# A conv block and a window-attention layer on one core: loads put ahead of stores, and four places in the strip order changed

## What is computed

```python
# L0: 1x1 conv (128->64), 3x3 grouped conv, 1x1 conv (64->128), each with its norm
h = relu(bn(conv(x, w1))); h = relu(bn(conv3x3(h, w2))); x = relu(bn(conv(h, w3)) + x)
# L1: windows of 7 x 7 = 49 tokens, shifted by 3; 8 heads of 16 channels
y = roll(ln(x) * w + b, (-3, -3)); win = windows(y)            # 8 windows in a strip of 7 rows
q, k, v = split(win @ qkv_w.T)
p = softmax(q @ k.T * scale + bias + mask)
x = x + roll(unwindow((p @ v) @ proj_w.T + proj_b), (3, 3))
z = ln(x) * w2 + b2
out = x + gelu(z @ fc1_w.T + fc1_b) @ fc2_w.T + fc2_b
```

## Time and profile before

| what | us |
|---|---|
| median of 3 executions | 4834.04 (4832.89 to 4839.28) |
| the profiled execution | 4831.1 |
| its span | 4829.0 |
| TensorE busy (matmul) | 4439.0 (92%) |
| ScalarE busy | 3444.2 (71%) |
| VectorE busy | 3214.6 (67%) |
| GpSimd busy | 2213.1 (46%) |

### The profile page before, as it was taken

One profiled execution on the slowest core, in us unless ns is written; L12 is line 12 of the kernel. 1 busy time (PEld: TensorE's weight loads), 2 busy tenths in 40 slices (PEclk: granted clock), 3 DMA queues, 4 the chain that ended last, 5 costly groups with the idle time before them and its releaser, 6 DMA issues.

```text
span 4829.0 us, 192181 instructions
## 1 busy us (share of the span) xinstructions
PE 4439.0 (92%) x71190; PEld 3280.4 (68%) x71190; DVE 3214.6 (67%) x7717; ACT 3444.2 (71%) x5644; POOL 2213.1 (46%) x3242
## 2 busy tenths in 40 slices
PE   8999996999999999999999999999999999999998
PEld 5666665666667666667666666666666666677665
DVE  4343435777777777777777777777777777777775
ACT  3444445777787777777777777777777777787776
POOL 4444433444444444444444444444444444444443
PEclk9999998999999999999999999999999999999999
DMA  4445441011001001000001001010010010000000
GB/s 141 148 146 158 147 137 42 27 28 28 27 27 27 26 27 28 26 27 27 27 27 28 27 27 27 27 27 27 27 28 27 27 28 27 27 27 27 26 27 24
DMA packets 298330, 218.64 MB, mean 45 GB/s; under 512 B 43377, under 2 KB 245518, under 8 KB 298190
## 3 DMA queue, kind: packets, MB, share of 16 engines
q1 hardware_dynamic: 294632, 215.41, 15.3%
q10 hardware_dynamic: 3558, 1.07, 0.1%
HBM read 110.73 MB, written 111.94 MB: 46 GB/s over the span
## 4 chain that ended last, share of the span: by engine, by line
issue 51%; POOL 30%; PE 15%; POOLq 2%; DVE 1%; ACT 0%; DMA 0%; DVEq 0%; ACTq 0%
POOL lnp L1145 15%; POOL sc L1222 12%; PE bank L501 6%; PE bank L514 4%; POOL res L1209 2%; PE bank L479 2%; PE bank L470 2%; POOL lnp L1197 1%; POOLq L1219 0%; PE bank L658 0%; POOLq L104 0%; POOLq L111 0%; PE bank L577 0%; POOLq L1195 0%; DVE sc L1051 0%
## 5 line engine op out<-in xcount | busy, mean ns | idle before, releaser
L1222 POOL TENSOR_TENSOR sc<-sc,mx 128x784 f32<-128x784 f32 x512 | 780.1, 1524 | 973.8 <-DVE mx L1057 973.8
L1209 POOL TENSOR_TENSOR res<-x,projb 98x512 f32<-98x512 f32 x256 | 327.5, 1279 | 1072.3 <-DVE x L1093 1072.3
L850 ACT ACTIVATE g<-bank,fc1b 128x392 f32<-128x392 f32 x1024 | 560.2, 592 | 244.7 <-PE bank L651 244.6
L658 PE MATMUL bank<-g,fc_sb 128*128 128x392 f32 x2048 | 716.7, 493 | 0.1
L914 DVE BATCH_NORM_STATS2 st<-x 98x6 f32<-98x128 f32 x2048 | 446.5, 281 | 260.7 <-DMA x<-x_scratch 252.0
L1076 DVE SCALAR_TENSOR_TENSOR xn<-x,lnp 98x128 f32<-98x128 f32 x1024 | 292.8, 348 | 446.7 <-POOL lnp L1145 445.8
L600 PEld LDWEIGHTS bank<-ident_sb,sc 128*113 128x113 f32 x4096 | 496.3, 177 | 106.7 <-DVE shared L1027 103.9
L633 PE MATMUL bank<-wproj,ot 128*98 128x128 f32 x2048 | 310.7, 299 | 269.2 <-DVE ot L1064 269.2
L1051 DVE TENSOR_TENSOR sc<-bank,shared 128x392 f32<-128x392 f32 x1024 | 528.3, 558 | 34.0 <-PE bank L587 33.8
L600 PE MATMUL bank<-ident_sb,sc 128*113 128x128 f32 x4096 | 541.6, 275 | 0.0
L577 PE MATMUL bank<-xt,wqkv 128*128 128x392 f32 x1024 | 480.0, 552 | 39.2 <-ACT xt L825 9.9
(11 more groups left out here) (105 smaller groups left out, 8451.2 us busy)
## 6 DMA issues: line engine op xcount, KB each, us to landing
x<-x_scratch SPq DMA_DIRECT2D x768, 49.0 KB
out_x<-y SPq DMA_DIRECT2D x672, 49.0 KB
xc_even<-in_x SPq DMA_DIRECT2D x128, 196.0 KB
shared<-in_x SPq DMA_DIRECT2D x128, 196.0 KB
x_scratch<-xc_even SPq DMA_DIRECT2D x128, 196.0 KB
x_scratch<-shared SPq DMA_DIRECT2D x128, 196.0 KB
x<-x_scratch SPq DMA_DIRECT2D x256, 38.5 KB
out_x<-y SPq DMA_DIRECT2D x224, 38.5 KB
```

The lines of the kernel that those rows point to most:

```text
L658: mm = nc.tensor.matmul(RC[:, 0:ST], fc2[:, c, :], g[:, c], start=c == 0, stop=c == HC - 1)
L850: nc.scalar.activation(g[:, j], ring[:, 0:ST], ACT.Gelu, bias=fc1b[:, j:j + 1]).then_inc(out_, 1)
L1222: P.tensor_tensor(out=s_r, in0=s_r, in1=m_r.to_broadcast([128, 2 * HEADS, N]), op=ALU.subtract).then_inc(sub_done, 1)
```

## The change

The change touches the order of work alone; no instruction is added or taken away.

- On SyncE a load goes one place further ahead: strip s+6 is loaded before strip s is stored (LEAD is 6). The wait for the wrapped strip's store and the two transfers behind it become a function of their own, `unwrap`, which is called one load and one store later.
- On TensorE the transposes of z (the MLP's input) move from the head of the stage to between values and the second project; row_sums moves between the two halves of mlp_out.
- On ScalarE zt_out goes behind k_out and v_out; reciprocals goes in front of the first half of the exponentials and of yt_out.
- On VectorE v_out goes in front of zt_rest, and ot_out in front of x2_norm.

```diff
-LEAD = 5
+LEAD = 6
...
@@ block.sync
-                if wraps:
-                    sp.wait_ge(y_out[u], 16 * MOVES * (STRIPS // 2) * (img + 1))
-                    below = WIN - SHIFT
-                    sp.dma_start(out[img, H - below:H], wrap_dram[img, 0:below]).then_inc(wrapped, 16)
-                    sp.dma_start(out[img, 0:SHIFT], wrap_dram[img, below:WIN]).then_inc(wrapped, 16)
+
+            def unwrap(img):
+                u = (STRIPS - 1) % 2
+                sp.wait_ge(y_out[u], 16 * MOVES * (STRIPS // 2) * (img + 1))
+                below = WIN - SHIFT
+                sp.dma_start(out[img, H - below:H], wrap_dram[img, 0:below]).then_inc(wrapped, 16)
+                sp.dma_start(out[img, 0:SHIFT], wrap_dram[img, below:WIN]).then_inc(wrapped, 16)
...
             for s in range(2, LEAD):
                 load_strip(0, s, s % 2)
+            load_strip(0, LEAD, LEAD % 2)
+            store_strip(0, 0, 0)
             with sp.Fori(0, B - 1) as img:
-                for s in range(STRIPS):
+                for s in range(1, STRIPS):
                     if s + LEAD < STRIPS:
                         load_strip(img, s + LEAD, (s + LEAD) % 2)
                     else:
                         load_strip(img + 1, s + LEAD - STRIPS, (s + LEAD) % 2)
                     store_strip(img, s, s % 2)
-            for s in range(STRIPS):
+                load_strip(img + 1, LEAD, LEAD % 2)
+                store_strip(img + 1, 0, 0)
+                unwrap(img)
+            for s in range(1, STRIPS):
                 if s + LEAD < STRIPS:
                     load_strip(B - 1, s + LEAD, (s + LEAD) % 2)
                 store_strip(B - 1, s, s % 2)
+            unwrap(B - 1)
...
@@ block.tensor, strips
+                if t.there():
+                    project(t, 0)
+                    values(t, 0)
+                    values(t, 1)
                 if t3.there():
                     pe.wait_ge(z_sb, t3.n + 1)
                     wait(pe, c_out, C_JOBS * t3.n)
                     to_channels(RC, z, c_full)
                 if t.there():
-                    project(t, 0)
-                    values(t, 0)
-                    values(t, 1)
                     project(t, 1)
...
                 if t3.there():
                     mlp_out(t3, 0)
+                if t1.there():
+                    row_sums(t1)
+                if t3.there():
                     mlp_out(t3, 1)
                 if t1.there():
-                    row_sums(t1)
                     attend(t1, 0)
                     attend(t1, 1)
...
@@ block.scalar, strips
-                if t3.there():
-                    zt_out(t3)
                 if t.there():
                     k_out(t)
                     v_out(t)
+                if t3.there():
+                    zt_out(t3)
...
+                if t1.there():
+                    reciprocals(t1)
                 if t.there():
                     exponentials(t, 0)
                 if t3.there():
                     yt_out(t3)
-                if t1.there():
-                    reciprocals(t1)
...
@@ block.vector, strips
+                if t.there():
+                    v_out(t)
                 if t3.there():
                     zt_rest(t3)
                 if t.there():
-                    v_out(t)
                     q_out(t)
...
+                if t1.there():
+                    ot_out(t1)
                 if t2.there():
                     x2_norm(t2)
-                if t1.there():
-                    ot_out(t1)
                 if t3.there():
                     y_sum(t3)
```

## The result

| what | before | changed |
|---|---|---|
| median, us | 4834.60 (4 runs) | 4522.72 (4518.32 to 4526.70, 4 runs) |
| ratio | | 0.9353, 95% interval 0.9337 to 0.9369 |
| span of the profiled execution, us | 4829.0 | 4516.2 |
| TensorE busy | 92% | 98% |
| mean granted clock | 0.973 | 0.992 |

What follows compares the result with a forecast made beforehand. A loop through VectorE and GpSimd set 15.01 us a strip; TensorE would then bound it at 14.30 + 0.22 = 14.52. Strips 125 plus wraps 174 give 299 us less: 4535 us, range 4504 to 4568 (chance 0.52).

Steps and rivals of the forecast that it cites:

- The wraps: SyncE, once in eight strips: loads in front and later wrap transfers remove 5.6 us at each of 31 wraps, 174 us.
- the step on VectorE's loop: VectorE: the loop loses 0.58 us of load wait and 1.09 us of z, to 13.34 us; second way round 13.62.
- 14.30 us: TensorE's own work per strip, taken as 15.01 us less 0.58 for ot and 0.13 for the copy of the keys.
- The price of a change of mode: TensorE, row sums between the halves of mlp_out: two more changes at 0.11 us each, 0.22 us a strip.
- the 0.13 of the wait: TensorE: transposes of z behind the values fill the 0.13 us wait for the copy of the keys.
- The balance of yt: ScalarE and TensorE, from mlp_out's start M: yt ready at M + 4.80 us, wanted at M + 4.83, so no stop.
- TensorE is a little freer: Rival: changes of mode cost nothing and yt is in time; 14.30 us a strip, 4479 us; chance 0.15.
- a thin cover fails: Rival: hidden waits for z's split or transposes wait for yt, 0.2 to 0.4 us; up to 4632 us; chance 0.20.
- only the wraps go: Rival: period stays 15.01 us because the drain or ScalarE takes the loads' gain; 4660 us; chance 0.06.
- the slower case: Rival: both mode changes stop TensorE 0.78 us each and bring the half clock; 16.77 us a strip, 5109 us; chance 0.03.
- the two last: Rivals: wraps stay while strips shrink, 4709 us, chance 0.02; or nothing happens, chance 0.02.

Runs made afterwards that it cites:

- wrap_inline: The whole change, with the wrap's wait and two transfers right behind the wrapped strip's store again; 4526.6 us, ratio 0.9364.
- loads_only: The kernel before with SyncE's part of the change alone (loads ahead of stores, wrap late), other engines as before; 4637.2 us, ratio 0.9592.
- z_before_ot: The whole change with x2_norm in front of ot_out on VectorE again; 4633.1 us, ratio 0.9577.
- order_only: The whole change with SyncE's part undone, so only the four changes of place; 4800.9 us, ratio 0.9933.
- z_before_ot_short_sub: The whole change with x2_norm before ot_out and GpSimd's second subtraction cut to one of 16 rows (softmax output differs); 4505.1 us, ratio 0.9315.
- attend_between: The whole change with attend too between the halves of mlp_out and the projection in front of mlp_to_tokens; 4500.2 us, ratio 0.9309.
- wrap_late_only: The kernel before with only the wrap's wait and two transfers issued one load and one store later; 4765.5 us, ratio 0.9854.
- sums_behind: The whole change with row sums (TensorE) and reciprocals (ScalarE) at their old places; 4635.0 us, ratio 0.9585.

## Why the prediction was right, and where it was only lucky

**The total and the period.** 299 us less were forecast, which gave 4535 us; the median is 4522.7, 312 us less. From the first to the last projection it is 306 us less. The other 6 to 7 us are 8.4 less ahead of the first projection (783.0 against 791.4 us) and 1.7 more behind the last; in the kernels here this first start varies between 783 and 791 us with no visible relation to the edit, so I don't count them as the change's. The period of 14.52 us is the one predicted.

**The wraps: right in size, wrong in cause.** The wraps cost 171 us before, where the prediction took 174, and all of it went. The ordinary stages gave the rest of the 306, 0.53 us each against the mean of 15.05; the strip that the prediction read, at 15.01, was a little short. But the text put the wraps' gain down to two edits together, and the late issue isn't needed: alone it gives 69 us, beside the loads in front it gives nothing (wrap_inline). What pays is where SyncE's idle time lies. The kernel before has as much of it:

```profile
2520.22 4.99 SPq L402 DMA_DIRECT2D out_x<-y  x5
```

The load of the earlier trace rows ends at 2515.42, so SyncE stood still for 4.8 us ahead of this store, and the load followed right behind the store. Now over 4 us lie ahead of the load, and the wrap's work fits in there.

**The ordinary stage: the step on VectorE's loop was incomplete.** It said that without the wait the loop is 0.58 us shorter, and without z ahead of ot a further 1.09. loads_only shows 0.1 for the first: the wait for the load had hidden the end of GpSimd's subtraction, and z now ran into it. The second is then worth 0.43 us in the whole change (z_before_ot), the rest of the way to 14.52. The loop was also only one of several. The runs show four rings of nearly the same length: SyncE's (15.04 us by order_only), VectorE's with the blocked z (14.95), ScalarE's with the late reciprocals (14.95), and one through the PSUM bank of the transposes of z (15.32), which exists only since ot and z stand ahead of y_sum. Each edit opens one, and the period comes down to 14.52, nearly TensorE's list, only when all four are open. The prediction costed the edits one by one against 14.30 us and gave nothing to reciprocals and transposes; left out, they cost 112 us (with the row sums) and 206 us. The sum came out because the end point, TensorE's list, was right to 0.08 us or a little more: z_before_ot_short_sub runs the same list in 14.44, and even there the projection follows ot at once.

**The price of a change of mode: too low, and offset.** From the start of mlp_out to that of the transposes of yt, the changed kernel takes 2510.44 - 2505.48 = 4.96 us in the strip shown, where it was 4.61. That is 0.35 for the two changes and not 0.22 (the second half of mlp_out takes 1.51 us to the start of attend, the first 1.41, the row sums 0.80 in place of 0.69). The prediction's 0.11 was the price of one way out of the narrow products, read at a single matmul. The trace has 0.09 us for each way in as well (the last matmul ahead of the row sums takes 0.42 us to the next start, the others 0.33), which the prediction had averaged away in its 0.34, and 0.1 us twice on the way out, at the row sums and at the first matmul behind them. Against this stands what the moved transposes of z gave: from the projection to the probability transposes it was 4.06 us and is 2514.78 - 2510.97 = 3.81, so 0.25 and not the 0.13 of the wait. The two errors cancel to 0.01 us, and that is luck. Two smaller ones cancel too (medians of some 100 strips): the probability transposes take 0.95 us in place of 0.86, and from the transposes of yt to the projection 0.70 us went where 0.58 were taken off. The rule of the Trainium skill, "TensorEngine Tiling (Array Packing)", section Key Properties, that a change of tiling mode drains TensorE, agrees with a cost that exists; by the sum above it is 0.35 us for two changes here.

**The balance of yt.** yt was to be ready at M + 4.80 and wanted at M + 4.83; it is ready at 2509.64 + 0.56 - 2505.48 = M + 4.72 and wanted at M + 4.96. No stop, as said.

**The rivals.** None came true. "TensorE is a little freer" is refuted by the 4.96 us, "a thin cover fails" by hidden, which waits for the split of z by 4 us in the whole run, and by the transposes of yt, which don't wait, "only the wraps go" by the period (loads_only, at 4637 us, comes nearest to it), and the slower case by the period and by the clock, which is 0.992 on average. No interval at a wrap is longer than the others now, and the ratio is 0.9353, which leaves nothing of the two last.

## What to carry to other kernels

When several engines work in a ring with periods within a few per cent, look for every ring before costing an edit: the four places together gave 34 us alone (order_only, 0.7%) and 114 us beside the loads in front (4637 to 4523 us), and leaving out one of them costs 110 to 206 us. A wait that is removed lets what stands behind it start earlier, and the question is what it then runs into; here it was another engine's access to the same memory. In a queue of transfers put first what someone waits for, so that the queue's idle time lies ahead of it: the irregular work here then cost nothing, wherever it stood.

## What the runs showed of the hardware

A VectorE instruction that reads both operands from SBUF took 1.05 us in place of 0.34 while a GpSimd subtraction ran; it shows as a longer instruction and not as a wait, so that no list of waits has it. One that reads PSUM and SBUF wasn't slowed (0.55 us in attend_between). A stop of TensorE of 2.8 us (wrap_late_only) was followed by the half clock, a projection of 2.02 us, in the strip shown, but not always: of its 31 wraps, with stops of 1.8 to 3.1 us, 15 have a projection of 2.02 us and 11 one of 1.11. In the kernel before, with stops of 2.8 to 4.1 us, 27 of 31 have 2.02. Stops of 0.69 us in every strip brought no half clock (sums_behind has a mean granted clock of 0.991).
